# First attention of a two-layer adaLN transformer: two half-seen key blocks of a slot merged into one before the exponentials, value differences, and another order of the work

## Chip, cores, metric

The kernel runs on one core of a Trainium2 chip. It is one launch, and the time is device microseconds of that launch: 2211.07 us, the median of three runs (2207.11 to 2211.23).

## What is computed

Two layers, each with adaptive layer norm, attention and a feed-forward part; x is (2, 512, 512) in float32. The change lies in the attention of layer 0 alone:

```python
G = 32 // 8                                   # 4 query heads for one key/value head
q = (x @ wq).reshape(B, S, 32, 128); k, v = ...reshape(B, S, 8, 128)
q, k = _rope(q, pos), _rope(k, pos)
scores = einsum('bqhgd,bshd->bhgqs', qg, k) * 128 ** -0.5
allowed = (j <= i) & (j > i - 128)            # sliding window of 128
attn = softmax(where(allowed, scores, neg))
out = einsum('bhgqs,bshd->bqhgd', attn, v)    # then out @ wo
```

With a window of 128 and blocks of 128 positions a query block qb sees parts of two key blocks: of its own those keys with j <= i, of the one before those with j > i within the block. At each of the 128 places in a block exactly one of the two is allowed. Query block 0 has only its own.

## The kernel before

**Work.** Float32 products are made of three products of rounded parts (high x high, high x low, low x high), in the helper mm3. Layer 0's attention runs over 8 key/value heads n and 2 batches b: a half is one (n, b), half = 2n + b, and has four slots, one for each query block qb; a slot handles the four query heads of the group at once. In a half, TensorE (PE) also projects the weights of the next half: the turns K, V, Q0, Q1, Vt (v is turned back by four transposes), Q2, Q3, which use banks 6 and 7 by turns. A projection into a bank waits (proj_free) until the product before last has been evacuated.

**One slot.** `scores` (PE, banks 0 and 1, 12 products of 256 columns, 128 for qb 0); `mask` (VectorE, DVE: adds the window mask, scales, writes probs in SBUF and the row's extreme in nmax); `exps` (ScalarE, ACT, in place, sum in den); `normalise` (DVE, reciprocal and a product in SBUF); `transposes` (PE: for both key blocks four transposes each into banks 2 and 3); `weights_high` (ACT, rounded copy pT_hi of each bank) and `weights_low` (DVE, the rest pT_lo); `sum_values` (PE, bank 4, three products a key block); `out_high`, `out_low` (ACT, DVE); `project_out` (PE, 12 products into bank 5); `gate_attention` (DVE, times the gate, into the single tile gated); `add_attention` (POOL, GpSimd: adds gated to x; the next gate_attention waits for it, attn0_added).

**Beside it.** `evacuate` (DVE: for K and Q three rope products out of PSUM, for Vt the low part v_lo); `rope_add` and `rope_low` (POOL) with `rope_high` (ACT) between them; `v_high` (ACT). Weights of the next head are split in high (ACT, weights_high0) and low parts (POOL, split_weights, six tiles), only in halves with b = 0; there POOL also splits the head's output weights in one operation of 128x2048 (`split_wo`, L679) at the start of the half, after ACT's copy of them (`out_weights_high`), which waits for the last project_out before.

**Order.** Each engine has its own list, written out by hand in a function kv_head(n, last) of each engine's block, and takes it strictly in order; engines wait for each other by counting semaphores (scores0, masked0, exp0, probs0, trans0, pT_hi_done, pT_split, pv0, ...). The list is run as kv_head(0), a hardware loop over heads 1 to 6, and kv_head(7, last) with b = 0 alone. The last half (LAST = 15) is written out behind it, among the work of the feed-forward part. DMA loads are issued by SyncE (SP).

Of the kernel before, what the change touches and what calls it, by code (L numbers as in the profile page):

```python
# [14 lines left out]
P = 128  # L15
# [50 lines left out]
def adaln_two_layers(nc, a, out):  # L66
# [8 lines left out]
    with ctx:  # L75
# [14 lines left out]
        cT = sb("cT", [P, 2, B, KT])  # L90
        silu_e = sb("silu_e", [P, 2, B, KT])
        silu_d = sb("silu_d", [P, 2, B, KT])
# [29 lines left out]
        v_hi = sb0("v_hi", [P, B, TB, HD], F32R)  # L122
        v_lo = sb0("v_lo", [P, B, TB, HD], F32R)
# [26 lines left out]
        gate_f0 = sb0("gate_f0", [P, B, D])  # L150
        qT_hi, qT_lo = (bq0_hi, bq1_hi), (bq0_lo, bq1_lo)
# [169 lines left out]
        kr_mm, kr_hi_done, kr_split, zeroed = sem("kr_mm"), sem("kr_hi_done"), sem("kr_split"), sem("zeroed")  # L321
# [91 lines left out]
        def _(sp):  # L413
# [44 lines left out]
            sp.dma_start(window[:], a["window_mask"]).then_inc(rope_loaded, 16)  # L458
            load_q(0)
# [209 lines left out]
        def _(pool):  # L669
# [73 lines left out]
            def kv_head(n, last):  # L743
                for b in range(1 if last else B):
                    half = 2 * n + b
                    split = b == 0 and not last
                    if b == 0:
                        split_wo(n)
                    if not (isinstance(n, int) and n == 0 and b == 0):
                        add_attention(4 * half - 1, TB * (1 - b) + 3)  # L750
                    rope_add(half + 1, "Q0", 1 - b)
                    if split:
                        split_weights(n + 1, (0,))
                    rope_low(half + 1, "Q0", 1 - b)
# [12 lines left out]
                    if split:  # L767
                        split_weights(n + 1, (2,))
# [32 lines left out]
            add_attention(4 * LAST - 1, 3)  # L801
            add_attention(4 * LAST, TB)
            add_attention(4 * LAST + 1, TB + 1)
            add_attention(4 * LAST + 2, TB + 2)
# [158 lines left out]
        def _(act):  # L963
# [55 lines left out]
            def v_high(half, b):  # L1019
                act.wait_ge(proj_done, TURNS * half + TURN["Vt"] + 1)  # L1020
                act.activation(v_hi[:, b].rearrange("p t d -> p (t d)"), bank[6 + (b + TURN["Vt"]) % 2][:], ACT.Copy).then_inc(v_hi_done, 1)
# [1668 lines left out]
```

## Time and profile before

| | |
|---|---|
| median of three runs | 2211.07 us |
| profiled execution, whole | 2213.3 us |
| its span | 2211.2 us |
| PE busy | 2153.0 us (97%) |
| DVE busy | 1702.5 us (77%) |
| ACT busy | 1461.9 us (66%) |
| POOL busy | 1225.7 us (55%) |
| granted TensorE clock, mean | 0.993 |

The span is from the first to the last instruction of the profiled execution. Busy time of an engine counts the time in which at least one of its instructions runs. The head loop of the first attention, with what leads into it, lies between some 62 and 690 us; the second layer's attention takes most of the time after 830 us.

### The profile page before, as it was taken

The numbers are of one execution on the slowest core, as the hardware profiler recorded it, in microseconds if no ns is written. First come the engines' busy times: TensorE is split into PE (matmuls) and PEld (weight loads), VectorE is DVE, ScalarE is ACT, GpSimd is POOL, SyncE is SP. The second block draws the span as 40 slices with busy tenths as digits, with TensorE's granted clock in tenths as the row PEclk, the third lists the DMA queues.
The fourth block names the chain that finished last, engine by engine and source line by source line (L and its number), as shares of the span: only waits on it lengthen the run. The fifth ranks groups of instructions, "written<-read, shape, count | busy, mean of one in ns | idle before, by whom it ended". The sixth has DMA issues, their size and how long they took to land.

```text
span 2211.2 us, 41636 instructions
## 1 busy us (share of the span) xinstructions
PE 2153.0 (97%) x11084; PEld 1653.9 (75%) x11084; DVE 1702.5 (77%) x3418; ACT 1461.9 (66%) x2868; POOL 1225.7 (55%) x1086
## 2 busy tenths in 40 slices
PE   7999999999999989999999999999999999999978
PEld 4888888888887657777777777777777777777655
DVE  6777677777777668888888888888888877788755
ACT  2444444444444668888888888888888877777732
POOL 4656665665663446666666666666666621455332
PEclk9999999999999999999999999999999999999998
DMA  7010010010004142111111111111111112343241
GB/s 244 20 48 29 19 47 28 19 47 28 19 14 125 36 175 83 48 43 48 47 48 42 48 48 46 49 42 49 47 48 42 48 49 59 105 120 90 80 126 39
DMA packets 125622, 132.46 MB, mean 60 GB/s; under 512 B 33277, under 2 KB 75805, under 8 KB 125548
## 3 DMA queue, kind: packets, MB, share of 16 engines
q1 hardware_dynamic: 121708, 118.97, 18.1%
q0 software_dynamic: 3840, 12.59, 1.9%
q8 instruction: 37, 0.61, 0.1%
q14 instruction: 37, 0.30, 0.0%
HBM read 101.59 MB, written 29.36 MB: 59 GB/s over the span
## 4 chain that ended last, share of the span: by engine, by line
PE 92%; DVE 4%; ACT 1%; DMA 1%; issue 1%; POOL 1%; SPq 0%; POOLq 0%; DVEq 0%; ACTq 0%
PE bank L2379 12%; PE bank L2386 11%; PE bank L2366 11%; PE bank L1951 9%; PE bank L1953 9%; PE bank L1952 9%; PE bank L2407 6%; PE bank L2298 5%; PE bank L2297 5%; PE bank L2296 5%; PE bank L2404 2%; PE bank L2087 2%; DVE rope_b L1479 1%; DVE rope_b L1480 1%; DVE rope_a L1478 1%
## 5 line engine op out<-in xcount | busy, mean ns | idle before, releaser
L1761 DVE TENSOR_REDUCE mcol<-bank 128x1 fp32r<-128x512 f32 x1024 | 694.2, 689 | 222.7 <-PE bank L2366 212.8
L2379 PE MATMUL bank<-q,k 128*128 128x512 f32 x1024 | 419.3, 410 | 2.0 <-DMA k<-kc_d 2.0
L2366 PE MATMUL bank<-km,q 128*128 128x512 f32 x1024 | 404.8, 396 | 3.2 <-DVE mcol L1761 1.6
L2386 PE MATMUL bank<-q,k 128*128 128x512 f32 x1024 | 407.0, 397 | 0.0
L2366 PEld LDWEIGHTS bank<-km,q 128*128 128x128 f32 x1024 | 316.3, 309 | 51.4 <-DVE mcol L1761 4.2
L1282 ACT ACTIVATE pT<-bank 128x512 f32<-128x512 f32 x512 | 284.9, 599 | 81.4 <-PE bank L2386 77.6
L1282 ACT ACTIVATE x<-bank 128x512 f32<-128x512 f32 x512 | 284.7, 600 | 80.7 <-PE bank L2386 77.1
L2379 PEld LDWEIGHTS bank<-q,k 128*128 128x128 f32 x1024 | 192.4, 188 | 128.9 <-ACT x L1282 44.3
L2386 PEld LDWEIGHTS bank<-q,k 128*128 128x128 f32 x1024 | 192.5, 188 | 32.4
L2298 PE MATMUL bank<-hT_hi,wr_lo 128*128 128x512 f32 x512 | 202.9, 396 | 0.0
L2296 PE MATMUL bank<-hT_hi,wr_hi 128*128 128x512 f32 x512 | 200.7, 392 | 1.6 <-DVE k L1634 1.6
L2297 PE MATMUL bank<-hT_lo,wr_hi 128*128 128x512 f32 x512 | 201.6, 394 | 0.0
L693 POOL TENSOR_TENSOR bq_lo<-rope_a,bq_hi 128x512 fp32r<-128x512 f32 x64 | 105.1, 1643 | 144.3 <-ACT bq_hi L1017 144.3
L837 POOL CAST pH<-x 128x512 f16<-128x512 f32 x96 | 58.7, 612 | 193.2 <-ACT x L1282 193.2
L1951 PE MATMUL bank<-hT_hi,w_hi 128*128 128x512 f32 x376 | 153.6, 408 | 6.9 <-DVE rope_b L1480 6.9
L1028 ACT ACTIVATE probs<-probs,nmax 128x256 f32<-128x256 f32 (+1 forms) x256 | 120.1, 475 | 57.8 <-DVE nmax L1490 57.8
L789 POOL TENSOR_TENSOR wr_lo<-wst,wr_hi 128x512 fp32r<-128x512 f32 x64 | 82.9, 1296 | 129.9 <-DVE wr_hi L1627 129.9
L685 POOL TENSOR_TENSOR rope_a<-rope_a,rope_b 128x512 f32<-128x512 f32 x80 | 111.4, 1392 | 67.2 <-DVE rope_b L1480 67.1
L1035 ACT ACTIVATE pT_hi<-bank 128x512 fp32r<-128x512 f32 x112 | 61.8, 596 | 131.1 <-PE bank L2087 131.1
L1953 PE MATMUL bank<-hT_hi,w_lo 128*128 128x512 f32 x376 | 147.2, 391 | 0.0
L1952 PE MATMUL bank<-hT_lo,w_hi 128*128 128x512 f32 x376 | 146.8, 390 | 0.0
L837 POOL CAST pH<-pT 128x512 f16<-128x512 f32 x96 | 58.6, 610 | 131.0 <-ACT pT L1282 131.0
(344 smaller groups left out, 5041.5 us busy)
## 6 DMA issues: line engine op xcount, KB each, us to landing
wst<-in_L_attn_Wq_rope SPq DMA_DIRECT2D x64, 256.0 KB, 3.0
o_d<-ost SPq DMA_DIRECT2D x512, 32.0 KB, 1.8
st_q<-in_L_attn_wq SPq DMA_DIRECT2D x8, 1024.0 KB, 7.8
st_wo<-in_L_attn_wo SPq DMA_DIRECT2D x8, 1024.0 KB, 5.2
km<-kc_d SPq DMA_DIRECT2D x256, 32.0 KB
q<-qc_d SPq DMA_DIRECT2D x256, 32.0 KB
k<-kc_d SPq DMA_DIRECT2D x256, 32.0 KB
wm<-in_L_wmod SPq DMA_DIRECT2D x6, 1024.0 KB, 10.5
```

The source lines that it names most:

```text
L1282: act.activation(PT[k % 2][:, s], bank[s % 4][:], ACT.Exp, scale=float((HD1 + ROPE) ** -0.5)).then_inc(exp1, 1)
L1761: dve.tensor_reduce(mcol[:, k % 2, i % 4, i // 4:i // 4 + 1], bank[4 + i % 2][:], AX.X, ALU.max, negate=True)\
L1951: pe.matmul(ps, lh_, rh, start=(i == 0), stop=False)
L1952: pe.matmul(ps, lh_, rl, start=False, stop=False)
L1953: e = pe.matmul(ps, ll, rh, start=False, stop=(i == n - 1))
L2296: pe.matmul(bank[6][:], wr_hi[:, par, kk], hT_hi[:, kk, at], start=(kk == 0), stop=False)
L2297: pe.matmul(bank[6][:], wr_hi[:, par, kk], hT_lo[:, kk, at], start=False, stop=False)
L2298: e = pe.matmul(bank[6][:], wr_lo[:, par, kk], hT_hi[:, kk, at], start=False, stop=(kk == KT - 1))
L2366: pe.matmul(bank[4 + i % 2][:], q2[:, k % 4, h, i % 4:S:4], km[:, b, h], start=True, stop=True).then_inc(max_mm, 1)
L2379: pe.matmul(bank[s % 4][:], k1[:, k % 2, t], q1[:, k % 4, h], start=True, stop=False)
L2386: pe.matmul(bank[s % 4][:], k2[:, k % 2, h, t], q2[:, k % 4, h], start=False, stop=True).then_inc(scores1, 1)
L2407: e = pe.matmul(rows(s), vp[:, k % 2, kb, h], PT[k % 2][:, s], start=(s < 4), stop=(s >= 4))
```

## The change

For slots with qb over 0, DVE takes the minimum of the two masked score blocks (scores are stored with a negative scale, so the masked entry is the huge one). There are then 128 columns for exponentials, normalise and transposes, and each slot's transposes use one bank, 2 or 3 by turns. With A the turned weights and O those of them that belong to the own block (A times the mask own), the sum is v_before A + (v_own - v_before) O. The differences dv of neighbouring v blocks are formed once a half. O's high part is a DVE product in weights_low, its low part a new POOL operation own_weights. masked0 and pT_split now count two a slot. kr_split becomes kv_split, with higher counts. The lists of all four engines get another order. cT, silu_e and silu_d move in SBUF.

```diff
@@ SP
+            sp.dma_start(own[:], a["own_block"]).then_inc(rope_loaded, 16)
@@ POOL
+            def own_weights(slot):
+                heads = lambda v: v.rearrange("p (h q) -> p h q", h=GQ)
+                mine = own[:].unsqueeze(1).broadcast_to([P, GQ, P])
+                pool.wait_ge(pT_split, 2 * slot + 1)
+                pool.tensor_tensor(heads(pT_lo[:, 1]), heads(pT_lo[:, 0].bitcast(F32)), mine, ALU.mult).then_inc(pT_split, 1)
@@ POOL, kv_head
                     if b == 0:
                         split_wo(n)
+                    rope_add(half + 1, "Q0", 1 - b)
                     if not (isinstance(n, int) and n == 0 and b == 0):
                         add_attention(4 * half - 1, TB * (1 - b) + 3)
-                    rope_add(half + 1, "Q0", 1 - b)
                     if split:
                         split_weights(n + 1, (0,))
                     rope_low(half + 1, "Q0", 1 - b)
+                    own_weights(4 * half + 1)
                     rope(half + 1, "Q1", 1 - b)
+                    if split:
+                        split_weights(n + 1, (1,))
                     rope(half + 1, "Q2", 1 - b)
+                    own_weights(4 * half + 2)
                     add_attention(4 * half, TB * b)
                     rope(half + 1, "Q3", 1 - b)
+                    own_weights(4 * half + 3)
+                    if split:
+                        split_weights(n + 1, (2,))
                     add_attention(4 * half + 1, TB * b + 1)
-                    if split:
-                        split_weights(n + 1, (1,))
...
                         rope_low(half + 2, "K", b)
-                    if split:
-                        split_weights(n + 1, (2,))
@@ ACT
+            def dv_high(half, b):
+                act.wait_ge(proj_free, TURNS * half + TURN["Vt"] + 1)
+                wait(act, pv0, 4 * half)
+                act.activation(dv_hi[:].rearrange("p t d -> p (t d)"), vT[:, 0:3 * P], ACT.Copy).then_inc(v_hi_done, 1)
...
-                c = slice(P, 2 * P) if qb == 0 else slice(0, 2 * P)
-                act.wait_ge(masked0, slot + 1)
+                c = slice(P, 2 * P) if qb == 0 else slice(0, P)
+                act.wait_ge(masked0, 2 * slot + 2)
...
-                for kb in range(1 if qb == 0 else 0, 2):
-                    e = act.activation(pT_hi[:, kb], bank[2 + kb][:], ACT.Copy)
-                e.then_inc(pT_hi_done, 1)
+                act.activation(pT_hi[:, 0], bank[2 + qb % 2][:], ACT.Copy).then_inc(pT_hi_done, 1)
@@ ACT, kv_head
                     weights_high(slot, 0)
+                    exps(slot + 1, 1)
+                    weights_high(slot + 1, 1)
                     out_high(slot)
                     if split:
                         weights_high0(n + 1, 0)
+                    v_high(half + 1, nb)
+                    rope_high(half + 1, "Q0", nb)
+                    exps(slot + 2, 2)
...
@@ DVE, evacuate "Vt"
+                    dve.wait_ge(v_hi_done, 2 * half + 1)
+                    dve.tensor_tensor(flat(v_lo[:, b]), ps[:, 0:3 * P], flat(v_hi[:, b]).bitcast(F32), ALU.subtract)
+                    dve.tensor_tensor(later, ps[:, P:4 * P], flat(v_hi[:, b]).bitcast(F32), ALU.subtract).then_inc(kv_split, 1)
+                    dve.wait_ge(kv_split, 2 * half + 1)
+                    dve.tensor_tensor(later, later, flat(v_lo[:, b]).bitcast(F32), ALU.subtract).then_inc(proj_free, 1)
+            def dv_low(half, b):
+                dve.wait_ge(v_hi_done, 2 * half + 2)
+                dve.tensor_tensor(dv_lo[:].rearrange("p t d -> p (t d)"), vT[:, 0:3 * P],
+                                  dv_hi[:].rearrange("p t d -> p (t d)").bitcast(F32), ALU.subtract).then_inc(kv_split, 1)
@@ DVE, mask
+                    e.then_inc(masked0, 1)
+                    dve.wait_ge(masked0, 2 * slot + 1)
+                    dve.tensor_tensor(probs[:, i, :, 0:P], probs[:, i, :, 0:P], probs[:, i, :, P:2 * P], ALU.min).then_inc(masked0, 1)
@@ DVE, weights_low
-                for kb in range(1 if qb == 0 else 0, 2):
-                    e = dve.tensor_tensor(pT_lo[:, kb], bank[2 + kb][:], pT_hi[:, kb].bitcast(F32), ALU.subtract)
-                e.then_inc(pT_split, 1)
+                if qb > 0:
+                    heads = lambda v: v.rearrange("p (h q) -> p h q", h=GQ)
+                    dve.tensor_tensor(heads(pT_hi[:, 1]), heads(bank[2 + qb % 2][:]), own[:].unsqueeze(1).broadcast_to([P, GQ, P]), ALU.mult)
+                dve.tensor_tensor(pT_lo[:, 0], bank[2 + qb % 2][:], pT_hi[:, 0].bitcast(F32), ALU.subtract)\
+                   .then_inc(pT_split, 2 if qb == 0 else 1)
@@ DVE, kv_head
                     mask(slot + 1, 1)
                     weights_low(slot, 0)
                     evacuate(half + 1, "Q0", nb)
+                    normalise(slot + 1, 1)
                     evacuate(half + 1, "Q1", nb)
+                    mask(slot + 2, 2)
                     out_low(slot)
-                    normalise(slot + 1, 1)
-                    mask(slot + 2, 2)
                     weights_low(slot + 1, 1)
                     evacuate(half + 1, "Vt", nb)
                     gate_attention(slot, b)
                     normalise(slot + 2, 2)
+                    evacuate(half + 1, "Q2", nb)
                     out_low(slot + 1)
-                    evacuate(half + 1, "Q2", nb)
                     mask(slot + 3, 3)
                     weights_low(slot + 2, 2)
+                    evacuate(half + 1, "Q3", nb)
+                    gate_attention(slot + 1, b)
                     normalise(slot + 3, 3)
-                    evacuate(half + 1, "Q3", nb)
                     out_low(slot + 2)
-                    gate_attention(slot + 1, b)
+                    if not last:
+                        evacuate(half + 2, "K", b)
                     weights_low(slot + 3, 3)
                     gate_attention(slot + 2, b)
-                    if not last:
-                        evacuate(half + 2, "K", b)
+                    out_low(slot + 3)
                     mask(slot + 4, 0)
-                    out_low(slot + 3)
+                    dv_low(half + 1, nb)
@@ PE
-                for kb in range(1 if qb == 0 else 0, 2):
-                    for h in range(GQ):
-                        e = pe.transpose(bank[2 + kb][:, h * P:(h + 1) * P], probs[:, qb % 2, h, kb * P:(kb + 1) * P], ident[:])
+                for h in range(GQ):
+                    e = pe.transpose(bank[2 + qb % 2][:, h * P:(h + 1) * P], probs[:, qb % 2, h, c], ident[:])
...
+                at = max(qb - 1, 0)
+                pe.matmul(bank[4][:], v_hi[:, b, at], pT_hi[:, 0], start=True, stop=False)
+                pe.matmul(bank[4][:], v_hi[:, b, at], pT_lo[:, 0], start=False, stop=False)
+                e = pe.matmul(bank[4][:], v_lo[:, b, at], pT_hi[:, 0], start=False, stop=(qb == 0))
+                if qb > 0:
+                    pe.wait_ge(pT_split, 2 * slot + 2)
+                    pe.matmul(bank[4][:], dv_hi[:, at], pT_hi[:, 1], start=False, stop=False)
+                    pe.matmul(bank[4][:], dv_hi[:, at], pT_lo[:, 1], start=False, stop=False)
+                    e = pe.matmul(bank[4][:], dv_lo[:, at], pT_hi[:, 1], start=False, stop=True)
@@ PE, kv_head
                     scores(slot + 1, half, b, 1)
                     transposes(slot, 0)
                     project(half + 1, "Q0", nb, n + b)
+                    project(half + 1, "Q1", nb, n + b)
+                    scores(slot + 2, half, b, 2)
+                    project(half + 1, "Vt", nb, n + b)
                     sum_values(slot, half, b, 0)
-                    project(half + 1, "Q1", nb, n + b)
-                    project(half + 1, "Vt", nb, n + b)
-                    scores(slot + 2, half, b, 2)
+                    transposes(slot + 1, 1)
                     project(half + 1, "Q2", nb, n + b)
-                    transposes(slot + 1, 1)
                     project_out(slot, n)
...
-                    transposes(slot + 3, 3)
                     if not last:
                         project(half + 2, "K", b, n + 1)
+                    transposes(slot + 3, 3)
                     project_out(slot + 2, n)
+                    scores(slot + 4, half + 1, nb, 0)
                     sum_values(slot + 3, half, b, 3)
-                    scores(slot + 4, half + 1, nb, 0)
```

## Rows read from the trace of the kernel before

**Rows 1.** The page, chain that ended last, by engine.
```profile
PE 92%; DVE 4%; ACT 1%; DMA 1%; issue 1%; POOL 1%; SPq 0%; POOLq 0%; DVEq 0%; ACTq 0%
```
**Rows 2.** One head by stretch: length; busy PE, PEld, DVE, ACT, POOL; clock; DMA.
```profile
188.00:272.00 84.00, 83.02 (x443) 70.78 (x442) 62.47 (x144) 39.32 (x106) 52.06 (x35) 1.00 0.10 32
```
**Rows 3.** Who waited for whom, 100 to 690 us: total us, times, longest.
```profile
PE bank L1951 <- DVE rope_b L1480: 6.6, 14, 0.5
```
**Rows 4.** Timeline of PE, one half with b = 0 (start, duration, instruction).
```profile
147.66 0.28 PE L1951 MATMUL bank<-kT_hi,bq_hi 128*128 128x256 f32 x1
149.09 0.60 PE L2087 MATMUL bank<-ident,probs 128*128 128x128 f32 x4
149.45 0.48 PE L1951 MATMUL bank<-hT_hi,w_hi 128*128 128x512 f32 x1
152.28 0.39 PE L1951 MATMUL bank<-pT_hi,v_hi 128*128 128x512 f32 x1
152.96 0.39 PE L1951 MATMUL bank<-hT_hi,w_hi 128*128 128x512 f32 x1
155.69 0.60 PE L2060 MATMUL bank<-ident,vT 128*128 128x128 f32 x4
156.04 0.36 PE L1951 MATMUL bank<-kT_hi,bq_hi 128*128 128x256 f32 x1
158.20 0.49 PE L1951 MATMUL bank<-hT_hi,w_hi 128*128 128x512 f32 x1 [0.49 <-DVE rope_b L1480]
161.05 1.03 PE L2087 MATMUL bank<-ident,probs 128*128 128x128 f32 x8
161.84 0.47 PE L1951 MATMUL bank<-wo_hi,oT_hi 128*128 128x512 f32 x1
...
189.74 0.28 PE L1951 MATMUL bank<-kT_hi,bq_hi 128*128 128x256 f32 x1
```
**Rows 5.** Groups by line and shape, 0 to 940 us.
```profile
L1028 ACT ACTIVATE probs<-probs,nmax 128x256 f32<-128x256 f32 x192 | 95.2, 503 | 25.3 <-DVE nmax L1490 25.3
L701 POOL TENSOR_TENSOR x<-x,gated 128x512 f32<-128x512 f32 x64 | 82.9, 1295 | 42.8 <-DVE gated L1537 42.7
L1035 ACT ACTIVATE pT_hi<-bank 128x512 fp32r<-128x512 f32 x112 | 61.8, 596 | 131.1 <-PE bank L2087 131.1
L1028 ACT ACTIVATE probs<-probs,nmax 128x128 f32<-128x128 f32 x64 | 25.0, 391 | 32.6 <-DVE nmax L1490 32.6
```
**Rows 6.** Timeline of DVE in that half; the last from a later half.
```profile
149.46 0.42 DVE L1490 CUSTOM_DVE_ANT_0 probs<-bank,window 128x256 f32<-128x256 f32 x1 [0.80 <-PE bank L1953]
150.84 0.69 DVE L1507 TENSOR_TENSOR pT_lo<-bank,pT_hi 128x512 fp32r<-128x512 f32 x1
158.91 1.63 DVE L1501 TENSOR_TENSOR probs<-probs,rden 128x1024 f32<-128x1024 f32 x1
...
188.03 0.69 DVE L1501 TENSOR_TENSOR probs<-probs,rden 128x512 f32<-128x512 f32 x1
```
**Rows 7.** Timeline of POOL in that half.
```profile
149.86 4.62 POOL L679 TENSOR_TENSOR wo_lo<-st_wo,wo_hi 128x2048 fp32r<-128x2048 f32 x1 [2.88 <-ACT wo_hi L1053]
158.16 1.30 POOL L693 TENSOR_TENSOR bq_lo<-rope_a,bq_hi 128x512 fp32r<-128x512 f32 x1
159.41 2.29 POOL L685 TENSOR_TENSOR rope_a<-rope_a,rope_b 128x512 f32<-128x512 f32 x1
```
**Rows 8.** Timelines of POOL and of DVE, around 314 us.
```profile
314.07 1.29 POOL L693 TENSOR_TENSOR kT_lo<-rope_a,kT_hi 128x512 fp32r<-128x512 f32 x1 [0.71 <-ACT kT_hi L1017]
...
314.23 1.69 DVE L1501 TENSOR_TENSOR probs<-probs,rden 128x512 f32<-128x512 f32 x1
```
**Rows 9.** Timeline of DVE: a normalise of 1024 columns that met nothing.
```profile
173.58 1.23 DVE L1501 TENSOR_TENSOR probs<-probs,rden 128x1024 f32<-128x1024 f32 x1
```
**Rows 10.** The chain that ended last, in order of time: the start.
```profile
4.63 8.44 DMA wm<-in_L_wmod
```
**Rows 11.** Timeline of DVE in the start: the evacuation of v.
```profile
44.46 0.69 DVE L1467 TENSOR_TENSOR v_lo<-bank,v_hi 128x512 fp32r<-128x512 f32 x1
```

More of the change, by code:

```diff
@@ L150, in adaln_two_layers @@
         gate_f0 = sb0("gate_f0", [P, B, D])
+        with ExitStack() as first:
+            sbs = sbuf_in(first)
+            cT = sbs("cT", [P, 2, B, KT])
+            silu_e = sbs("silu_e", [P, 2, B, KT])
+            silu_d = sbs("silu_d", [P, 2, B, KT])
+        dv_lo = sb0("dv_lo", [P, TB - 1, HD], F32R)
         qT_hi, qT_lo = (bq0_hi, bq1_hi), (bq0_lo, bq1_lo)
@@ L801, in _ @@
             add_attention(4 * LAST - 1, 3)
+            own_weights(4 * LAST + 1)
             add_attention(4 * LAST, TB)
+            own_weights(4 * LAST + 2)
             add_attention(4 * LAST + 1, TB + 1)
+            own_weights(4 * LAST + 3)
             add_attention(4 * LAST + 2, TB + 2)
@@ L1064, in kv_head @@
                         weights_high0(n + 1, 0)
+                    v_high(half + 1, nb)
+                    rope_high(half + 1, "Q0", nb)
+                    exps(slot + 2, 2)
                     if split:
                         weights_high0(n + 1, 1)
-                    exps(slot + 1, 1)
-                    rope_high(half + 1, "Q0", nb)
-                    weights_high(slot + 1, 1)
-                    v_high(half + 1, nb)
-                    exps(slot + 2, 2)
+                    if split:
+                        weights_high0(n + 1, 2)
                     rope_high(half + 1, "Q1", nb)
@@ L1074, in kv_head @@
                     weights_high(slot + 2, 2)
-                    exps(slot + 3, 3)
                     rope_high(half + 1, "Q2", nb)
-                    out_high(slot + 2)
-                    weights_high(slot + 3, 3)
-                    rope_high(half + 1, "Q3", nb)
-                    if split:
-                        weights_high0(n + 1, 2)
                     if split:
                         weights_high0(n + 1, 3)
+                    exps(slot + 3, 3)
+                    out_high(slot + 2)
+                    rope_high(half + 1, "Q3", nb)
+                    weights_high(slot + 3, 3)
                     out_high(slot + 3)
+                    if not last:
+                        rope_high(half + 2, "K", b)
+                    dv_high(half + 1, nb)
                     exps(slot + 4, 0)
@@ L1118, in _ @@
             v_high(0, 0)
+            dv_high(0, 0)
             mod_rows(0, (3,))
@@ L1471, in evacuate @@
                 if name == "V":
+                    wait(dve, kv_split, 2 * half)
                     dve.tensor_copy(vT[:], ps[:]).then_inc(proj_free, 1)
@@ L1595, in _ @@
             norm_split(0, 1, (6,))
+            dv_low(0, 0)
             norm_split(0, 1, (7,))
@@ L2072, in scores @@
                     pe.wait_ge(rope_split, 5 * half + 5)
-                wait(pe, masked0, slot)
+                wait(pe, masked0, 2 * slot if qb == 1 else 2 * slot - 1)
                 c = slice(P, 2 * P) if qb == 0 else slice(0, 2 * P)
@@ L2094, in sum_values @@
                 wait(pe, oT_split, slot)
-                mm3(bank[4][:], [(v_hi[:, b, qb - 1 + kb], v_lo[:, b, qb - 1 + kb], pT_hi[:, kb], pT_lo[:, kb])
-                                 for kb in range(1 if qb == 0 else 0, 2)], pv0)
+                at = max(qb - 1, 0)
[7 more added lines that the diff above has]
+                    e = pe.matmul(bank[4][:], dv_lo[:, at], pT_hi[:, 1], start=False, stop=True)
+                e.then_inc(pv0, 1)
             def project_out(slot, n):
@@ L2176, in kv_head @@
                     project_out(slot + 3, n)
+                    if isinstance(n, int) and n == 0 and b == 0:
+                        pe.wait_ge(gate_ready, 1)
             pe.wait_ge(ident_loaded, 32)
```

46 lines of the change are left out of this document (22 added, 24 removed).

## Prediction

> **What bounds the kernel now.** First the chain that ended last: 92% of it is TensorE (PE) and 4% VectorE (DVE) [rows 1]. Then busy time by stretch: in one whole turn of the head loop (two halves, 84 us) PE is busy 83.0 of 84 us, DVE 62.5, GpSimd (POOL) 52.1, ScalarE (ACT) 39.3 [rows 2]. So in the first attention, where all of the change lies, PE sets the time and the others must deliver to it. Third, the waits between 100 and 690 us: PE stands idle there almost only once a half, 0.5 us, 14 times, until DVE has evacuated a rope product [rows 3]. That is also the only place where the old order was too tight. Fourth, the timeline of one half, which gives the price of each PE step: a half runs from 147.66 to 189.74, 42.08 us [rows 4]. In that half the reader is to see scores at 147.66, four transposes in 0.36 us (149.09 to 149.45), a projection in 2.83 us, three value products in 0.68 us, the four v transposes in 0.35 us, scores, the wait of 0.49 us before 158.20, and eight transposes in 0.79 us (161.05 to 161.84).
>
> **What the change takes from PE.** A slot with qb over 0 has four transposes in place of eight: 0.79 - 0.36 = 0.43 us [rows 4]. There are 3 such slots in each of 16 halves. 15 halves run in the head loop: 45 x 0.43 = 19.4 us, all on the path. The 3 of the last half lie between other work of the chain: 1.3 us. Score and value products keep their number (6 products a slot, now with differences of v). The wait of 0.49 us goes if nothing new stands there, because scores, v transposes, the first value sum and four transposes (1.45 + 0.35 + 0.68 + 0.36 = 2.8 us) now lie between projections Q1 and Q2, where 2.0 us lay (155.69 to 158.20, less the wait): 15 x 0.49 = 7.4 us. Together -28.1 us, and a half of PE without any wait is 42.08 - 0.49 - 1.29 = 40.3 us.
>
> **What it does to the others.** ACT: exponentials of 128 columns for 256, 4 x (0.50 - 0.39), and one copy of 0.60 us less a slot [rows 5]: about 1.0 us less a slot, but ACT was at 47%, so this is worth nothing by itself; it only shortens chains. The new dv_high copy (384 columns, not in the trace; between the 0.39 us exponential of 128 and the copy of 0.60 us of 512, I take 0.5) lies in the same slack. DVE: the min of two 128 x 512 operands in SBUF is not in the trace; nearest is the normalise of 128x512, also both operands in SBUF, 0.69 us when alone [rows 6]; bounds 0.69 and, with waits, 1.69; I take 0.69 plus the waits told below. The normalise shrinks from 1.23 us [rows 9] to 0.69. The product with the own-block mask takes the place of the second pT_lo subtraction, also from PSUM, 0.69 for 0.69. Per half the v part grows from one 0.68 us to about 0.55 + 0.55 + 0.55, and dv_low adds 0.55: +1.5 us. In sum DVE goes from 31.2 to about 33 us of a 40.3 us half before any waiting. POOL gets three own_weights a half; nearest row the 128x512 add, 1.3 us [rows 5], bounds 1.3 and the 2.3 us of one that had to wait [rows 7]: +3.9 us on 26.
>
> **The step that decides: who may read SBUF.** At 158.16 POOL starts a 1.30 us operation; DVE's normalise starts at 158.91 and takes 1.63 us instead of 1.23, ending 1.08 us after POOL's end; POOL's next, issued at 159.41, takes 2.29 instead of 1.30, so it began only when DVE was done [rows 6, 7]. Again: POOL at 314.07 for 1.29 us, the 128x512 normalise at 314.23 takes 1.69 for 0.69 [rows 8]. So a DVE operation with both operands in SBUF and a POOL operation exclude each other, and the later one waits for the end of the other's instruction. DVE operations that read PSUM do not show it (the four masks and pT_lo, 149.46 to 151.5, run at full pace inside POOL's 4.62 us split of wo) [rows 6, 7]. The change raises the number of such DVE operations in a half from 4 to 9 and puts the first of them, the min of slot 1, right behind the masks.
>
> The Trainium skill, page "SBUF — State Buffer", the list under the diagram of its two sides, calls the shared port pair "an exclusive lock, not a bandwidth split", held for the whole instruction, and counts a DVE operation with two SBUF inputs against a POOL operation that reads SBUF. By that rule the 4.62 us split would be held to its end, as the sum below has it; if only pieces of the length that the rows show (1.3 us) were held, the sum would be that of the first rival. The trace agrees for the short ones and has no long one that a DVE operation met.
>
> **Half b = 0, counted from the start of its scores (147.66 = 0).** POOL splits wo, released by ACT's copy, from 2.20 to 6.82 [rows 7]. DVE masks slot 1 from 1.80 to 3.18 [rows 6]. The min is ready at 3.2 and waits for POOL to 6.8: done 7.5. Behind it on DVE stand pT_lo of slot 0 (to 8.1) and the evacuation of Q0 (three operations, 0.70 apart: to 10.2; its product was there at 4.8). ACT does exponentials of slot 1 from 7.5 to 9.1. POOL's rope_add of Q0 starts at 10.2, when Q0 is out, before DVE's normalise of slot 1 (the reciprocal stands ahead of it, 0.2 us), so the normalise waits to 11.5 and ends at 12.1; then Q1's evacuation, 12.1 to 14.2. PE without waits would begin Q2 at 1.43 + 0.36 + 2 x 2.83 + 2.84 + 0.1 (the first products behind transposes come a little further apart) = 10.4, but Q2 needs Q1's bank: 14.2. That is 3.8 us (taken in three places: v transposes, transposes of slot 1, Q2). Going on in the same way, the first output product waits 0.25 for out_low, the own part of slot 2's sum 0.25 (POOL: rope_low, then split 1, rope of Q2, own_weights), the last output product 0.3 (gate_attention waits for an addition that now stands behind own_weights and split 2 on POOL). Sum 4.6 us; 8 such halves: +36.8.
>
> **Half b = 1.** No split of wo, but at its start the last split of q weights (up to 4 us in, 1.3 us pieces). The min ends at 4.0 to 4.7. Rope_add of Q0 against the normalise of slot 1 is the same as above, 1.1 us: Q1 is out at 11.1 to 11.4 against 10.4 wanted, 0.7 to 1.0. Min of slot 3 meets rope_low of Q2 nearly at the same moment; whoever comes first, sum_values of slot 2 is late, 0.1 to 1.3. Together 0.8 to 2.4, I take 1.6; 7 such halves: +11.2.
>
> **Start.** The evacuation of v is on the chain (44.46, 0.69 us, then the norm's operations on DVE) [rows 11]. There the growth of DVE's part, 1.5 us, counts in full. The added load of own (64 KB behind the rope tables) and the moved tensors I cost at nothing: the first long load, for which the chain waits from 4.63 to 13.07 [rows 10], is issued ahead of it, and own is wanted by POOL only in the second slot. If that is wrong, the load of the q weights behind it comes later by the time of one issue, some tenths of a microsecond.
>
> **Sum** against the profiled execution, 2213.3 us (2.1 us around a span of 2211.2): -28.1 + 36.8 + 11.2 + 1.5 = +21.4, so 2234.7. The median of the runs shown is 2.2 us below the profiled one: 2232 us. The forecast's own range is 2216 to 2241: the b = 1 term from 5.6 to 16.8, and the b = 0 term from 26 (the min is let in after two thirds of its wait) to 40.
>
> **Rivals.**
> *The long split does not hold DVE off* (the min gets in between, or another order of starts lets it). For: no row shows a wait over 1.1 us. Against: every row shows a wait to the end of the instruction. Then a b = 0 half costs what a b = 1 half does, 15 x 0.8 to 15 x 1.6 in place of 48: 2213.3 - 28.1 + 12 to 24 + 1.5 - 2.2 = 2197 to 2209, say 2204: slightly faster.
> *PE gets all it is owed*, no new wait: 2213.3 - 28.1 + 1.5 - 2.2 = 2184. This ends on the other side by one mechanism: the half is bound by PE's own work as soon as min, pT_lo and the evacuation of Q0 are done by 7.8 us after the start, and the normalise before rope_add. For: PE is on 92% of the chain. Against: the collision of rope_add with the normalise needs no assumption; it already happens one step later now (158.16 against 158.91).
> *DVE becomes the bound.* 33 us of work, 9 operations that can each wait up to 1.3, and the semaphore waits fixed by order: with 5.6 us a b = 0 half and 2.4 a b = 1 half, 44.8 + 16.8 = 61.6: 2213.3 - 28.1 + 61.6 + 1.5 - 2.2 = 2246.
> *The work saved on PE is not on the path.* Against: rows 3 show PE waiting 0.5 us a half only. It has no chance of its own.
>
> **Chances.** Forecast 0.50, long split does not hold 0.22, PE gets all 0.13, DVE the bound 0.12, else 0.03. No change means within 0.2% (4.4 us, about what a measurement of this kernel can tell from none): 0.09, from the upper end of the first rival and the low end of the forecast. Faster 0.31 (second rival whole, most of the first), slower 0.60. The range that should hold 8 in 10 reaches into both sides: 2190 to 2248.
>
> **What would show it.** Right: in the profile after, the min of slot 1 in every other half takes some 4 us and begins some 1 us after POOL's 4.6 us operation; DVE's evacuation of Q0 starts at +7.5 to 8 there; PE has idle time of 1 us and more before v transposes, before transposes of slot 1 and before Q2, about 4 us in b = 0 halves, 1 to 2 in b = 1 halves, released by DVE; halves of about 44.9 and 41.9 us. Transposes: 256 for 448. Wrong: mins of 0.7 to 1.7 us everywhere and halves near 41 us (first rival), or 40.3 (second). If PE's idle time was released by POOL's own_weights, the step that failed is its place in POOL's order. Any change after 760 us would be outside all of this.

## The result, and the profile after

| | before | after |
|---|---|---|
| median of the runs, us | 2211.15 (2207.11 to 2213.23, 4 runs) | 2247.74 (2245.04 to 2251.29, 4 runs) |
| ratio to before, 95% interval | | 1.0167 [1.0154, 1.0180] |
| profiled execution, its span, us | 2213.3, 2211.2 | 2251.3, 2249.2 |
| transposes of the first attention | 448 | 256 |
| 14 half turns of the head loop, us | 589.9 | 619.5 |

The change costs 36.6 us, where 21 were forecast: the sign was right, the size too small by 15 us. The forecast's own range, 2216 to 2241 us, does not hold the measured 2247.7. The page of after, its busy time and its chain (shares of the span):

```profile
PE 2163.5 (96%) x10892; PEld 1637.9 (73%) x10892; DVE 1796.9 (80%) x3514; ACT 1425.4 (63%) x2836; POOL 1281.6 (57%) x1134
...
PE 67%; POOL 14%; issue 12%; DVE 4%; ACT 1%; DMA 1%; SPq 1%; POOLq 0%; DVEq 0%; ACTq 0%
```

Against [rows 1] PE has fallen from 92% of the chain to 67%, and POOL is on it with 14%: the end is no longer set by PE alone.

Two half turns of after by busy time, the first with a fallen clock, the second without, both with b = 0, and all 14 half turns in one row; then the same 14 of before (us of the stretch, busy us of each engine, granted clock, DMA):

```profile
141.99:189.17 47.18, 43.25 (x210) 35.14 (x209) 39.39 (x79) 19.01 (x52) 30.71 (x20) 0.96 0.07 23
231.97:276.29 44.32, 41.38 (x210) 34.03 (x209) 37.67 (x79) 18.80 (x52) 30.26 (x20) 1.00 0.07 24
99.39:718.84 619.45, 587.14 (x2916) 477.72 (x2914) 523.87 (x1090) 242.15 (x703) 411.96 (x287) 0.99 0.12 36
```
```profile
98.83:688.76 589.93, 581.33 (x3083) 494.99 (x3082) 443.31 (x1008) 273.89 (x731) 359.83 (x245) 1.00 0.13 38
```

PE had 8.6 us without work in the 14 halves of before and has 32.3 now. DVE is busy 80 us more. Some 36 us of that is work and short waits: e7 below, where the long waits are gone, is busy 479.1 us in its 14 halves, against 443.3 before. The other 45 us are time inside instructions that wait. The waits of PE in the same stretch (line, what it waited for: us in total, times, longest us), first of after, then of before:

```profile
PE bank L1994 <- DVE rope_b L1509: 12.0, 14, 1.4
PE bank L2103 <- DVE rope_b L1509: 6.8, 7, 1.0
PE bank L2130 <- DVE probs L1540: 6.4, 8, 2.0
PE bank L2144 <- POOL pT_lo L710: 3.9, 10, 0.4
```
```profile
PE bank L1951 <- DVE rope_b L1480: 6.6, 14, 0.5
PE bank L1951 <- DVE gated L1537: 2.0, 1, 2.0
```

Where 8.6 us of waits stood, 29.1 stand in these four lines. The ledger, from the spans (38.0 us in all):

| stretch | before | after | difference |
|---|---|---|---|
| to the head loop's first marker | 98.83 | 99.39 | +0.6 |
| 7 halves with b = 0 | 295.5 | 320.3 | +24.8 |
| 7 halves with b = 1 | 294.4 | 299.2 | +4.7 |
| from there to the second layer's head loop | 115.0 | 116.1 | +1.0 |
| second layer's head loop | 1290.7 | 1296.7 | +6.0 |
| the end | | | +0.9 |

(The marker is the first score product of the slot with qb = 0, near the end of a half. In before 41.99 to 42.08 us lie between two markers, and 43.11 before the last. The first marker stands near the end of the loop's first half with b = 0, so that the eighth such half belongs to the first row.) The halves with b = 1 take 42.60 to 42.80 us. Those with b = 0 take, in their order, 47.18, 44.32, 44.41, 44.34, 46.06, 47.20 and 46.77.

### The profile page after: what moved, and what is told of

It reads as the page before. It is cut to its first block, busy times and chain, and to the rows that moved or that the text cites. A ratio compares the mean times of both kernels' runs of the same rounds, so it can differ in the third digit from the quotient of the medians.

```text
span 2249.2 us, 41579 instructions
## 1 busy us (share of the span) xinstructions
PE 2163.5 (96%) x10892; PEld 1637.9 (73%) x10892; DVE 1796.9 (80%) x3514; ACT 1425.4 (63%) x2836; POOL 1281.6 (57%) x1134
## 4 chain that ended last, share of the span: by engine, by line
PE 67%; POOL 14%; issue 12%; DVE 4%; ACT 1%; DMA 1%; SPq 1%; POOLq 0%; DVEq 0%; ACTq 0%
PE bank L2430 12%; PE bank L2417 11%; PE bank L2437 10%; PE bank L2458 6%; PE bank L2349 5%; PE bank L2347 5%; PE bank L2348 5%; POOL rope_a L691 3%; POOL bq_lo L699 3%; POOL x L714 2%; PE bank L2455 2%; POOL w_lo L681 2%; PE bank L1994 2%; PE bank L1996 1%; PE bank L1995 1%
## 5 line engine op out<-in xcount | busy, mean ns | idle before, releaser
L2430 PEld LDWEIGHTS bank<-q,k 128*128 128x128 f32 x1024 | 192.2, 188 | 128.3 <-ACT x L1306 44.4
L1052 ACT ACTIVATE probs<-probs,nmax 128x128 f32<-128x128 f32 x256 | 99.8, 391 | 89.2 <-DVE probs L1532 83.6
L699 POOL TENSOR_TENSOR bq_lo<-rope_a,bq_hi 128x512 fp32r<-128x512 f32 x64 | 88.8, 1388 | 56.1 <-ACT bq_hi L1036 56.1
L710 POOL TENSOR_TENSOR pT_lo<-pT_lo,own 128x512 fp32r<-128x512 f32 x48 | 61.8, 1287 | 101.5 <-DVE pT_lo L1548 101.0
```

Source lines behind the costliest of these rows:

```text
L2430: pe.matmul(bank[s % 4][:], k1[:, k % 2, t], q1[:, k % 4, h], start=True, stop=False)
```

## The forecast chain, in one half with b = 0

The scores of this half's slot 1 start at 240.25 us. DVE of after:

```profile
243.09 0.42 DVE L1525 CUSTOM_DVE_ANT_0 probs<-bank,window 128x256 f32<-128x256 f32 x1
...
243.55 4.06 DVE L1532 TENSOR_TENSOR probs<-probs 128x512 f32<-128x512 f32 x1
247.53 0.68 DVE L1548 TENSOR_TENSOR pT_lo<-bank,pT_hi 128x512 fp32r<-128x512 f32 x1
248.13 0.67 DVE L1507 TENSOR_TENSOR rope_a<-bank,rope_cos 128x512 f32<-128x512 f32 x1
...
250.45 1.66 DVE L1540 TENSOR_TENSOR probs<-probs,rden 128x512 f32<-128x512 f32 x1
252.04 0.68 DVE L1507 TENSOR_TENSOR rope_a<-bank,rope_cos 128x512 f32<-128x512 f32 x1
```

POOL of after beside it:

```profile
242.44 4.62 POOL L685 TENSOR_TENSOR wo_lo<-st_wo,wo_hi 128x2048 fp32r<-128x2048 f32 x1 [3.26 <-ACT wo_hi L1075]
250.29 1.28 POOL L691 TENSOR_TENSOR rope_a<-rope_a,rope_b 128x512 f32<-128x512 f32 x1 [3.23 <-DVE rope_b L1509]
```

PE of after:

```profile
250.26 0.66 PE L2103 MATMUL bank<-ident,vT 128*128 128x128 f32 x4 [0.96 <-DVE rope_b L1509]
...
252.25 0.65 PE L2130 MATMUL bank<-ident,probs 128*128 128x128 f32 x4 [0.63 <-DVE probs L1540]
254.25 0.50 PE L1994 MATMUL bank<-hT_hi,w_hi 128*128 128x512 f32 x1 [1.35 <-DVE rope_b L1509]
```

The reader is to see that the min starts 1.1 us after POOL's split and ends half a microsecond after it: 4.06 us for 0.69 of work, the masks ahead of it, which read PSUM, at full pace. Counted from the scores: min done +7.4 (forecast 7.5), Q0's evacuation from +7.9 (8.1), Q1's from +11.8 (12.1), Q2 at +14.0 (14.2), and three waits of PE in the three places named. All seven such halves between the markers have a first min of 4.06 to 4.12 us, and the eighth, ahead of the first marker, one of 4.83.

## Experiments

Each ratio is to runs of the kernel before made beside the experiment, with medians of 2210.3 to 2211.7 us.

**1. The long split cut in four.** The same work, in four instructions of 128x512. e1:

```diff
-pool.tensor_tensor(wo_lo[:], st_wo[:], wo_hi[:]..., ALU.subtract).then_inc(wo_split, 1)
+for h in range(GQ):
+    e = pool.tensor_tensor(wo_lo[:, h], st_wo[:, h], wo_hi[:, h]..., ALU.subtract)
+e.then_inc(wo_split, 1)
```

> The changed kernel, with POOL's 128x2048 split of wo cut into four 128x512 operations, same place, same work. Theory (the min waits for the end of a whole POOL instruction): the min of slot 1 in b = 0 halves falls from 4.06 us to under 1.9, those halves from 44.3-47.2 us to 41-42.5, TensorE's granted clock does not fall in them, the whole is 2212 to 2222 us. Rival (the min waits because POOL's queue as a whole is late, or for data): mins stay near 4 us, time 2244 to 2250.

Measured 2214.57 us (2209.67 to 2216.09, 10 runs), ratio to before 1.0011 [1.0001, 1.0020]. DVE and POOL of e1, at the place shown above:

```profile
237.52 0.74 DVE L1534 TENSOR_TENSOR probs<-probs 128x512 f32<-128x512 f32 x1
238.18 0.68 DVE L1550 TENSOR_TENSOR pT_lo<-bank,pT_hi 128x512 fp32r<-128x512 f32 x1
239.18 0.69 DVE L1509 TENSOR_TENSOR rope_a<-bank,rope_cos 128x512 f32<-128x512 f32 x1 [0.32 <-PE bank L1998]
```
```profile
236.42 5.51 POOL L686 TENSOR_TENSOR wo_lo<-st_wo,wo_hi 128x512 fp32r<-128x512 f32 x4 [3.25 <-ACT wo_hi L1077]
```

The min now gets in between two pieces: 0.74 us, and the four pieces together pay 5.51 for 4.62. Halves with b = 0 fall to 40.8 us with the clock at full; those with b = 1 stay at 42.8. So the lock (DVE held off for the whole of one 4.6 us POOL instruction), with all it brings behind it, is 33 of the 36.6 us.

**2. The lock alone, in the kernel before.** To the old kernel one min a half is added behind the masks of slot 1 (its result is written where nobody reads it before it is overwritten), without and with the split cut:

```diff
+if qb == 1:
+    dve.wait_ge(masked0, slot + 1)
+    dve.tensor_tensor(pT_lo[:, 0]..., probs[:, i, :, 0:P], probs[:, i, :, P:2 * P], ALU.min)
```

> The kernel before, with one added DVE operation a half: behind the masks of slot 1 the minimum of its two score blocks is written to a part of pT_lo that nobody reads then. Nothing else is changed, the result neither. Theory (lock held for the whole 4.62 us split): the added operation takes 0.69 to 1.3 us in b = 1 halves and 4.0-4.3 in b = 0 halves; there Q2 waits 1.8 to 2.5 us longer; 2225 to 2237 us. If the clock falls after that wait, more. Rival (the lock is let go inside a long instruction, the slowdown came from the new order): under 2214 us.

> As e4_min_in_before, with the split of wo in four operations. Theory: the added operation takes under 1.9 us everywhere; 2210 to 2216 us. Rival: as e4_min_in_before.

Measured 2253.80 (2249.07 to 2256.10, 4 runs; ratio 1.0190 [1.0170, 1.0211]) and 2222.61 (2219.83 to 2224.50, 4; 1.0054 [1.0036, 1.0072]). Both lie above what I expected, by 17 and by 7 us. e4, timelines of DVE, of POOL and of PE, and two of its halves with b = 0:

```profile
247.07 4.00 DVE L1495 TENSOR_TENSOR pT_lo<-probs 128x512 fp32r<-128x512 f32 x1
251.00 0.68 DVE L1510 TENSOR_TENSOR pT_lo<-bank,pT_hi 128x512 fp32r<-128x512 f32 x1
```
```profile
245.97 4.56 POOL L679 TENSOR_TENSOR wo_lo<-st_wo,wo_hi 128x2048 fp32r<-128x2048 f32 x1 [2.88 <-ACT wo_hi L1053]
```
```profile
251.93 0.47 PE L1954 MATMUL bank<-pT_hi,v_hi 128*128 128x512 f32 x1 [3.37 <-DVE pT_lo L1510]
```
```profile
146.91:194.03 47.12, 43.25 (x222) 36.42 (x221) 36.05 (x74) 21.05 (x54) 26.72 (x17) 0.96 0.07 23
236.94:282.69 45.75, 41.88 (x222) 35.30 (x221) 36.47 (x74) 21.05 (x54) 26.69 (x17) 1.00 0.06 23
```

One instruction of 0.7 us of work, set at the wrong place, costs the old kernel 43 us; 31 of them go when POOL's neighbour is cut. The wait is not where I expected it: PE waits 3.4 us before the first value product of slot 0, for the pT_lo that stands on DVE right behind the added min, and the wait before Q2 stays at 0.5 us as in [rows 3]. The 12 us that stay in e5 have the same place. In its halves with b = 1 (42.9 us) PE waits 0.55 us for this pT_lo, where it did not wait before, and in those with b = 0 (42.6) its value product starts 0.3 us late; the wait before Q2 is again 0.5 us. And e4 shows a second thing: of six halves with the same waits five take 45.74 to 45.77 us and one 47.12, and that one has the granted clock 0.96.

**3. The rest of the order, step by step.** e2 is e1 with POOL's rope_add of Q0 held until DVE's normalise of slot 1 is done (otherwise rope_add is ready first, by the 0.2 us of the reciprocal that stands ahead of the normalise); e7 is e2 with POOL's rope_low of Q2 behind the min of slot 3:

```diff
+pool.wait_ge(probs0, 4 * half + 2)                     # e2 and e7
 rope_add(half + 1, "Q0", 1 - b)
...
-rope(half + 1, "Q2", 1 - b)                            # e7
+rope_add(half + 1, "Q2", 1 - b)
+pool.wait_ge(masked0, 2 * (4 * half + 3) + 2)
+rope_low(half + 1, "Q2", 1 - b)
```

> As e1_pieces, and POOL's rope_add of Q0 waits until the normalise of slot 1 is done (it started first and held it up by 1.1 us). Theory: in b = 1 halves the wait of TensorE before projection Q2 (0.7 to 1.4 us) goes, those halves fall from 42.75 to 41.5-42; b = 0 halves change little, as the last piece already stands where rope_add stood; 5 to 10 us under e1_pieces. Rival (DVE is simply full): no gain over e1_pieces, the wait turns up at the next step.

> As e2_pieces_wait, and POOL's rope_low of Q2 waits until the min of slot 3 is done (it began just ahead of it and made it 1.83 us long in b = 1 halves). Theory: that min takes 0.69 us everywhere, b = 1 halves go from 42.13 to 41.2, the whole from 2206.5 to 2199-2202. Rival (own_weights, which now stands later behind rope_low, takes the wait over): halves of 42 us, 2205 to 2208.

Measured: e2 2206.54 (2204.46 to 2210.35, 10; 0.9980 [0.9970, 0.9989]), e7 2204.78 (2200.79 to 2205.91, 11; 0.9978 [0.9969, 0.9987]). Halves with b = 1 go from 42.8 (e1) to 42.1 (e2, where two of seven already take 41.2) and to 41.2 (e7); the min of slot 3 there goes from 1.83 to 0.69 us. Two halves of e7:

```profile
178.26:219.44 41.18, 40.92 (x210) 34.09 (x209) 34.40 (x79) 15.98 (x49) 27.69 (x21) 1.00 0.13 39
219.44:260.39 40.95, 40.90 (x210) 34.03 (x209) 34.32 (x79) 18.67 (x52) 30.15 (x23) 1.00 0.08 26
```

PE works 40.9 of 41.0 us: this is the kernel that the change aimed at. It does DVE's same work in 34.4 us, where after shows 37.7: a busy DVE was no bound. e7 was expected at 2199 to 2202 us. Its 14 halves take 3.3 us less than e2's in the profiled executions, because two of e2's were already short and its own halves with b = 0 became 0.1 us longer; the median fell by 1.8. Its second layer's loop takes 1296.8 us, which is the next experiment.

**4. The places of the tensors.** With cT and the two silu tensors moved, every tensor behind them lies 192 bytes lower (in the change, some by further multiples of 512 bytes). e6 makes only that move, in the kernel before; e13 adds only an unused tensor of 64 bytes to it; e10 makes e6's move and takes 64 bytes more away, so that all lies 256 bytes lower:

```diff
-cT = sb("cT", [P, 2, B, KT])                           # e6 and e10: these three
+cT = sbs("cT", [P, 2, B, KT])                          # behind gate_f0
-mean_var = sb("mean_var", [P, NT, 2])                  # e10
+mean_var = sb0("mean_var", [P, NT, 2])                 # e10
+sb("pad", [P, 16])                                     # e13
```

> The kernel before, with only the three small tensors cT, silu_e and silu_d moved as in the change, so that all that lies behind them in SBUF stands 192 bytes lower. The second layer's attention loop (first to last km product) took 1290.7 us before and 1296.7 to 1297.2 in every kernel made from the changed one. Theory (the addresses do it): that stretch takes 1296 to 1298 us here, and the whole 2215 to 2219. Rival (it comes from elsewhere in the change, such as the place of the code): 1289 to 1292, whole 2208 to 2214.

> The kernel before with an unused tile of 64 bytes put in front of layer 0's tiles, nothing moved otherwise, all behind stands 64 bytes higher. 64 and -192 have the same place within 128 and 256 bytes. Theory: as e6, halves near 42.47 us, 2217 to 2223. Rival (the move of cT and the silu tiles costs, not the shift): as before, 2208 to 2213.

> The kernel before with the tensors of e6 moved and mean_var (64 bytes) moved behind layer 0's tiles as well, so that the tiles behind stand 256 bytes lower instead of 192. Theory (a tile's place within 128 or 256 bytes sets the pace of the matmuls): as the kernel before, halves of 42.07 us, second loop 1290 to 1292, 2208 to 2213. Rival (any move costs, or moving the start's tensors costs by itself): as e6, halves of 42.47, 2217 to 2223.

| | shift, bytes | us | ratio | a half | second loop |
|---|---|---|---|---|---|
| before | 0 | 2210.29, 2211.66 | | 42.07 | 1290.7 |
| e6 | -192 | 2221.23 (5 runs) | 1.0048 [1.0034, 1.0062] | 42.46 | 1295.4 |
| e13 | +64 | 2222.41 (5 runs) | 1.0053 [1.0039, 1.0066] | 42.45 | 1296.7 |
| e10 | -256 | 2209.84 (11 runs) | 0.9993 [0.9984, 1.0002] | 42.07 | 1291.5 |

PE's timeline, the first and the last of nine products of one projection in e13, and the same products of before:

```profile
153.05 0.39 PE L1952 MATMUL bank<-hT_hi,w_hi 128*128 128x512 f32 x1
...
154.91 0.39 PE L1954 MATMUL bank<-hT_hi,w_lo 128*128 128x512 f32 x1
```
```profile
152.96 0.39 PE L1951 MATMUL bank<-hT_hi,w_hi 128*128 128x512 f32 x1
...
154.78 0.39 PE L1953 MATMUL bank<-hT_hi,w_lo 128*128 128x512 f32 x1
```

Eight steps in 1.86 us against 1.82: 0.2325 us each against 0.2275, at full clock and with no wait. No instruction differs. So the move alone costs the old kernel 11 us, in both loops, by the pace of matmuls. It is not the pace of all of them. Added up from start to start over one turn (two halves), e6 takes 0.8 us more than before; 0.6 of that lies in the 144 projections (hT times weights), 0.1 in the output products, nothing in the score and value products. In the second layer's loop the projections of hT take 357.5 us for 351.5, and its other products together no more than before. hT itself lies ahead of the moved tensors; the weights lie behind them.

**5. What the places cost the changed kernel.** e8 pads the changed kernel so that the second layer's tensors lie as before; e14 moves mean_var too and pads, so that the first layer's tensors lie 256 bytes lower and the second's as before; e9 is e7 with e8's pad, e11 is e7 with e14's edit, e15 is e1 with it:

```diff
-F_PAD = 256
+F_PAD = 304                                            # e8, e9
+F_PAD = 320                                            # e14, e11, e15
-mean_var = sb("mean_var", [P, NT, 2])                  # e14, e11, e15
+mean_var = sb0("mean_var", [P, NT, 2])
```

> The changed kernel, with the pad in front of the tiles of the second layer 192 bytes longer, so that these tiles stand where they stood before the change. Theory (addresses): the second layer's loop takes 1290 to 1292 us for 1296.7, the whole 2240 to 2244 for 2248; the first attention unchanged. Rival: 1296 to 1298 and 2246 to 2250.

> e7_min_first and e8_pad together: the changed kernel with the split of wo in four, rope_add of Q0 behind the normalise, rope_low of Q2 behind the min, and the longer pad. If the parts add up: 2193 to 2197 us. If the pad does nothing: as e7_min_first.

> e9_best with mean_var moved behind layer 0's tiles too (those tiles then 256 bytes lower than before the change instead of 192) and the pad of the second layer's tiles 64 bytes longer. Theory: halves of 40.5 to 40.8 us for 40.95 and 41.2, 2190 to 2193 us. Rival (the place matters in the second layer only): 2196 to 2199.

> The changed kernel with the addresses alone mended: mean_var behind layer 0's tiles (those then 256 bytes lower than before the change, not 192) and the pad of the second layer's tiles 64 bytes longer. Everything else, the 4.62 us split too, as in the change. If what the moved tensors cost alone (+10.9 us) is their share in the change: 2235 to 2239 us, b = 0 halves without a fall of the clock 44.0, b = 1 halves 42.3, second loop 1290 to 1294. Rival (DVE and POOL set those halves, so TensorE's pace is worth nothing in them; only the second layer gains): 2241 to 2244.

> e14_only_aligned with the split of wo in four. If the two causes add up and there is no third: e1_pieces (2214.6) less 8 to 11, 2203 to 2207; b = 0 halves 40.4, b = 1 halves 42.4. Rival (the slots of DVE and POOL set the b = 1 halves): b = 1 halves stay at 42.8, 2206 to 2210.

| | us | ratio | halves b = 0, b = 1 | second loop |
|---|---|---|---|---|
| e8 | 2246.62 (5 runs) | 1.0166 [1.0152, 1.0180] | 44.4 (two), 46.1 to 47.2 (five), 42.8 (one 41.9) | 1291.9 |
| e14 | 2249.19 (5) | 1.0176 [1.0162, 1.0190] | 44.1 (two), 45.1 to 47.5 (the others), 42.67 | 1293.5 |
| e15 | 2209.86 (11) | 0.9991 [0.9980, 1.0002] | 40.66, 42.66 | 1291.5 |
| e9 | 2197.49 (5) | 0.9946 [0.9932, 0.9960] | 40.95, 41.2 | 1292.9 |
| e11 | 2196.22 (5) | **0.9926 [0.9913, 0.9940]** | 40.79, 40.82 | 1293.8 |

In kernels without the long lock the places are worth a good part of e6's 11 us: by the ratios to before, 4 us from e1 to e15, 7 from e7 to e9 and 11 from e7 to e11. Of these e15 came out as its rival had it (halves with b = 1 near 42.7, 2206 to 2210), e9 0.5 us above its range, and e11 with the halves as expected but the whole 3 us above. In the changed kernel the places bring nothing that can be told, and neither expectation for e14 held. Its undisturbed halves are 0.3 us shorter and its second loop 3 us. But leave the last half with b = 0 aside, which is longer in before too: in four of the other six the granted clock falls, where it does in three of after. In e8 it does in four as well, and e8's whole did not gain the 4.8 us of its second loop. Over all its runs e14 has a mean granted clock of 0.987 to 0.989, where after has 0.990 to 0.994. So the 11 us are not a term that could be added to the sum, and the change's 36.6 us can't be split into exact shares. e11 is the best version that was run: 15 us under the kernel before, with the merge kept.

**6. The new item order.** e12 is e1 with the old order of items on all four engines, the merge kept (own_weights behind each rope on POOL):

> The merging of the blocks without the new order: e1_pieces (split of wo in four) with the four engines' lists as in the kernel before, own_weights behind rope_low of Q0, rope of Q2 and rope of Q3, dv_high and dv_low at the end of the half. Theory (the new order is needed, because between Q1's and Q2's projection only 2.0 us of other work stood and DVE now has a min more): TensorE still waits 0.5 us and more before Q2, halves of 41.3 to 42.5, 2212 to 2225. Rival (the order is worth nothing): as e1_pieces, 2212 to 2216, with halves of 41 to 42.8.

Measured 2299.88 (2296.66 to 2300.92, 5 runs; 1.0403 [1.0389, 1.0417]): I had missed by 75 us. Waits of PE in 107 to 580 us, and the largest in PE's timeline:

```profile
PE bank L2146 <- POOL pT_lo L712: 28.0, 10, 2.8
PE bank L2141 <- DVE pT_lo L1550: 7.4, 15, 0.6
PE bank L1996 <- DVE rope_b L1511: 4.7, 10, 0.5
```
```profile
192.74 0.50 PE L2146 MATMUL bank<-pT_hi,dv_hi 128*128 128x512 f32 x1 [2.80 <-POOL pT_lo L712]
```

The 2.8 us are one wait a half, in the value sum of slot 2. The timelines give its chain: POOL's own_weights of slot 2 stands behind rope_low of Q2, this waits 3.1 us for ACT's rope_high of Q2, and in the old list that stands behind the exponentials of slot 3, which need the min of slot 3. The clock falls too: in the profiled execution 12 of the 14 halves behind the first have the granted clock 0.96 or lower. So the merge needs its operations placed with care, and with these lists it costs 85 us more than e1. That no other place for own_weights would do in the old order is not shown, for only this one was run, and the new order was not run without the merge.

## Why the prediction came out as it did

The forecast was 2232 us, and 2247.7 came. The wider range, 2190 to 2248, holds that by 0.3 us, and only because its upper end was set by a rival (DVE as the bound) whose mechanism did not appear: luck. The chain of causes was right for the larger part of the cost. Two terms of the sum failed: the moved tensors, put at nothing, and the new waits of PE, priced as idle time alone, as if the granted clock would not fall behind them. A third, a half with b = 1, was put 0.8 us too short.

**Right: the step that decides.** DVE and POOL, each with operands in SBUF (DVE with both), exclude each other for the whole instruction, the min of slot 1 meets the 4.62 us split in each half with b = 0, and rope_add goes before the normalise. Each time along that half came within 0.3 us, and e1, e4 and e5 show the cause by taking it away and by adding it elsewhere. The first rival (the long split doesn't hold DVE off) fell with the mins of 4.06; "PE gets all it is owed" with the waits. The rival that came nearest in size, DVE as the bound (2246 against 2247.7), has the wrong mechanism: e7 does the same DVE work in halves of 41 us.

The Trainium skill, page "SBUF — State Buffer", the list under the diagram of its two sides, has the lock held for the whole instruction. The trace now agrees for a long one too: 3.4 us of waiting to the end of a 4.62 us instruction, seven times of seven.

**Wrong: "the moved tensors I cost at nothing".** They cost 10.9 us alone in the kernel before (e6), and 6.0 us of the ledger lie in the second layer's loop, where no item was changed; e8, with the places of the second layer as before, has 1291.9 us there for 1296.7. The prediction also said that any change after 760 us would be outside all of it; there was one. In the first attention the undisturbed halves with b = 0 are 0.3 us shorter with the places mended (e14), but e14 as a whole gained nothing.

**Missing from the sum: the clock.** It stood at 1.00 in the rows that I had read of before, and I did not ask what the new waits would do to it. PE of after, in the half of 47.18 us:

```profile
164.25 0.50 PE L1994 MATMUL bank<-hT_hi,w_hi 128*128 128x512 f32 x1 [1.35 <-DVE rope_b L1509]
...
165.05 0.61 PE L1994 MATMUL bank<-hT_hi,w_hi 128*128 128x512 f32 x1
165.46 0.63 PE L1995 MATMUL bank<-hT_lo,w_hi 128*128 128x512 f32 x1
...
168.45 0.41 PE L1996 MATMUL bank<-hT_hi,w_lo 128*128 128x512 f32 x1
168.70 0.39 PE L1994 MATMUL bank<-wo_hi,oT_hi 128*128 128x512 f32 x1
```

Windows of 5 us at that place, and at the same place of the half of 44.32 us:

```profile
165.00:170.00 5.00, 5.00 (x16) 3.91 (x16) 4.93 (x11) 3.12 (x11) 4.27 (x4) 0.66 0.00 0
255.00:260.00 5.00, 5.00 (x22) 3.78 (x22) 4.93 (x11) 3.13 (x11) 4.28 (x4) 1.00 0.00 0
```

After three waits within five microseconds the products come 0.42 us apart for 3.4 us, the lower of the two levels (1.2 for 2.4 GHz), then 0.23 again. That makes the output products late by 1.4 us. In two of the three such halves (47.18 and 47.20) the min of slot 3 then falls together with rope_low (1.83 us for 0.69, as in every half with b = 1); in the third (46.06) it does not. Together they pay 7.4 us above the undisturbed ones.

The seventh half with b = 0, 46.77 us, is another case. Its clock falls only at its end, behind a wait of 2.0 us. In before the clock falls in the same half (43.11 us for 42.07), also behind a wait of 2.0 us; stretches of 2 us there, in before and in after:

```profile
684.00:686.00 2.00, 2.00 (x6) 1.54 (x6) 0.04 (x1) 0.00 (x0) 2.00 (x2) 0.50 1.05 387
```
```profile
715.00:717.00 2.00, 2.00 (x7) 1.52 (x6) 1.29 (x2) 0.08 (x1) 0.71 (x2) 0.50 1.04 383
```

So a fallen clock stood in the trace of before, which the prediction passed over. e14 shows what that half costs without one: 45.14 us at clock 1.00, with the same waits.

**Sizes.** An undisturbed half with b = 0 was 44.35 where 44.9 was forecast: 4 us less over seven. The three smaller waits of the forecast (0.25, 0.25 and 0.3 us, behind Q2) do not appear as waits in these halves. A half with b = 1 was 42.74 where 41.9 was forecast: 6 us more. By the experiments the latter is 40.8 of PE, 0.7 for rope_add ahead of the normalise (e1 to e2), 0.9 for the min of slot 3 behind rope_low (e2 to e7), and up to 0.4 of places (e7 to e11): the two collisions cost 1.6, as I took them. What was off is the floor of a half, 40.8 and not the 40.3 of the forecast, and the 0.4 of the places. In a whole turn, two halves, of e11 the 42 value products take 10.4 us from start to start where they took 9.6 before. In part the sum's first product comes at a wider step behind scores and behind v's transposes (0.29 and 0.32 us for 0.23), in part the own part of slot 2 starts some 0.4 us late in halves with b = 0. The transposes save 2.4 us and not 2.6. That is nearly all of the 0.5 us a half.

The stretch to the first marker holds the start and one half with b = 0, for which the forecast had 1.5 and 2.8 us; 0.6 were seen. That can't be told: leaving e12 out, the first marker lies between 94 and 104 us over the profiled executions.

**Open.** Whether the period of the places is 128 or 256 bytes (e13 and e6 fit both), and which of the moved tensors it is about, though the projections pay most of it. Why the clock falls in some halves with b = 0 and not in others that agree with them to some 0.02 us up to that point. And why the parts don't add: e14's lower mean clock suggests that what the places give back goes into further halves with a fallen clock, but no run holds the clock fixed.

## What to carry to other kernels

Before a DVE operation with both operands in SBUF is added, list the POOL instructions that run at its time, and cut the longest: four pieces for one cost POOL 0.9 us and gave back 33 us here. An edit that only frees or moves an SBUF tensor can cost time (11 us here): compare the distance between matmuls before and after, and keep all that stands behind it at the same place within 256 bytes. Where PE stands at 99% busy, price each new wait twice, once as idle time and once for the chance that the granted clock falls behind it.

## What the runs showed of the hardware that was not expected

- A shift of all later tensors by 64 or by -192 bytes slows the fp32 projections (hT times weights, 512 columns) from 0.2275 to 0.2325 us (2%) and the whole kernel by 0.5%, score and value products not at all; a shift by -256 bytes costs nothing (0.9993 [0.9984, 1.0002]).
- A wait of DVE for POOL to end shows as a longer instruction and as busy time, not as a wait: a min of 4.06 us for 0.69, with no idle time before it, and 45 us of such time in the loop of after.
- The granted clock fell to half for 3.4 us after waits of 0.96, 0.63 and 1.35 us in a stretch otherwise full, in three of six halves with the same waits; in e4 in one of six, behind one wait of 3.4 us; and at the end of the last half with b = 0 behind one of 2.0 us, in before too.
